# A four-layer network on one Trainium2 core: layer 3 gets its gate weights by DMA through memory, its output biases on VectorE, and eight units of first products ahead of the gate

## What is computed

```python
x_flat = x.transpose(0, 2, 3, 1).reshape(-1, c)
scores = softmax(x_flat @ gate_w + gate_b, -1)
top_v, top_i = top_k(scores, 2)
top_w = softmax(top_v, -1)                         # two weights for each pixel
present = (top_i[:, :, None] == arange(4)[None, None, :]).any(0)   # [2, 4], over all pixels
coef = einsum('ke,kbhw->ebhw', present, wmap)      # wmap: top_w as [2, b, h, w]
hdn = relu(einsum('bchw,edc->ebdhw', x, w1) + b1)
y   = einsum('ebdhw,eod->ebohw', hdn, w2) + b2
out = einsum('ebohw,ebhw->bohw', y, coef)
```

## Time and profile before

| | us |
|---|---|
| median of 3 runs | 5612.05 (5609.07 to 5618.05) |
| the profiled execution | 5612.2 |
| its span in the trace | 5610.3 |
| start of the last image's tail to the first second product | 4527 to 4596 |
| the loop over units, to the last matmul | 4596 to 5606 |

### The profile page before, as it was taken

One profiled execution on the slowest core, in us unless ns is written; L12 is line 12 of the kernel. 1 busy time (PEld: TensorE's weight loads), 2 busy tenths in 40 slices (PEclk: granted clock), 3 DMA queues, 4 the chain that ended last, 5 costly groups with the idle time before them and its releaser, 6 DMA issues. The chain is left out here.

```text
span 5610.3 us, 78498 instructions
## 1 busy us (share of the span) xinstructions
PE 4822.8 (86%) x28644; PEld 3822.7 (68%) x28644; DVE 4242.3 (76%) x4727; ACT 3094.3 (55%) x6442; POOL 2967.4 (53%) x3548
## 2 busy tenths in 40 slices
PE   4888888888888888888888877788887979999999
PEld 2666666666666666666666654466665859999998
DVE  1999999999999999999999986666666643333333
ACT  3776777777777777777777743222232323333332
POOL 3776777777777777777777744545443400000000
PEclk8999999999999999999999988798887979999999
DMA  2001000000000010000000012102010101000100
GB/s 74 1 15 29 9 9 10 9 22 22 10 9 10 19 29 14 9 9 10 9 9 10 5 41 80 43 19 75 28 37 15 64 25 33 28 26 28 33 26 22
DMA packets 88527, 136.75 MB, mean 24 GB/s; under 512 B 5285, under 2 KB 85185, under 8 KB 88141
## 3 DMA queue, kind: packets, MB, share of 16 engines
q1 hardware_dynamic: 88140, 131.72, 7.3%
HBM read 89.23 MB, written 42.47 MB: 23 GB/s over the span
## 5 line engine op out<-in xcount | busy, mean ns | idle before, releaser
L743 DVE TENSOR_TENSOR_SCAN a_h<-a_dA,pw 128x771 f32<-128x771 f32 x1152 | 2014.1, 1751 | 121.7 <-PE pw L450 120.8
L599 ACT ACTIVATE a_dA<-a_dt,a_Aneg 128x384 f32<-128x384 f32 x2304 | 1345.2, 607 | 152.4 <-DVE a_h L743 147.4
L461 PEld LDWEIGHTS pw<-g_ident,a_h 128*128 128x128 f32 x6912 | 783.5, 142 | 618.2 <-DVE a_acc L762 268.1
L881 POOL TENSOR_SCALAR a_dBT<-a_dtxT,a_BC 128x768 f32<-128x768 f32 x1152 | 1025.0, 907 | 298.4 <-PE pw L450 213.7
L461 PE MATMUL pw<-g_ident,a_h 128*128 128x128 f32 x6912 | 980.6, 279 | 227.7 <-DVE a_acc L762 157.8
L450 PE MATMUL pw<-g_ident,a_dBT 128*128 128x128 f32 x6912 | 954.2, 275 | 4.8 <-POOL a_dBT L881 4.8
L762 DVE SCALAR_TENSOR_TENSOR a_acc<-pw,a_BC,a_acc 128x768 f32<-128x768 f32 x912 | 913.8, 1002 | 50.9 <-PE pw L461 46.7
L450 PEld LDWEIGHTS pw<-g_ident,a_dBT 128*128 128x128 f32 x6912 | 801.5, 142 | 6.6 <-POOL a_dBT L881 5.5
L1895 DVE TENSOR_TENSOR d_hf<-d_hf,ps 128x384 f32<-128x384 f32 x288 | 159.1, 554 | 566.0 <-ACT d_hf L1825 555.5
L833 POOL TENSOR_TENSOR a_xin<-a_xin,a_tm 128x384 f32<-128x384 f32 x432 | 433.0, 1002 | 34.3 <-ACT a_tm L520 9.0
L893 POOL TENSOR_TENSOR a_acc<-a_acc,a_tm 128x768 f32<-128x768 f32 x168 | 307.0, 1827 | 161.1 <-ACT a_tm L613 160.2
(11 more groups left out here) (243 smaller groups left out, 9365.2 us busy)
## 6 DMA issues: line engine op xcount, KB each, us to landing
b_xs<-x SPq DMA_DIRECT2D x36, 576.0 KB, 4.0
a_xs<-in_x SPq DMA_DIRECT2D x24, 576.0 KB, 4.0
x<-a_xs SPq DMA_DIRECT2D x24, 576.0 KB, 3.0
b_x<-x SPq DMA_DIRECT2D x24, 576.0 KB, 4.6
e_xs<-x SPq DMA_DIRECT2D x24, 576.0 KB, 3.9
out<-e_xs SPq DMA_DIRECT2D x24, 576.0 KB, 3.0
a_sx<-in_x SPq DMA_DIRECT2D x54, 192.0 KB, 2.4
x<-b_x SPq DMA_DIRECT2D x16, 576.0 KB, 3.0
```

The costliest lines, as they stand in the source:

```text
L461: t = e.transpose(m["pw2"][:, c * 128:(c + 1) * 128], m[f"a_h{g % 2}"][:, c // 2, first_col(c) + tb * 128:first_col(c) + (tb + 1) * 128], ...
L599: e.activation(dA[:, first_col(c):first_col(c) + T], m[f"a_dt{k % 2}"][:, c, :], ACT.Exp, scale=m["a_Aneg"][:, c, n:n + 1]).then_inc(s["a_ ...
L743: e.tensor_tensor_scan(m[f"a_h{g % 2}"][:, p % 3, :], m[f"a_dA{pi % NDA}"][:], m[f"pw{pi % 2}"][:, COL:COL + PAIR], 1.0, ALU.mult, ALU.add ...
L881: t = e.tensor_scalar(m[f"a_dBT{g % 2}"][:, tb, :], m[f"a_dtxT{o}"][:, tb, :], m[f"a_BC{o}"][:, tb, n:n + 1], 1.0, ALU.mult, ALU.mult)
```

## The change

- **Weights.** The gate's result lies as `e_co`, expert by expert. TensorE turns it once, with three transposes, into 96 x 384 in `ps3`; ScalarE copies that to `e_cT`; one DMA writes it to a new tensor `cw` in memory (144 KB). For each chunk one DMA reads 4 x 384 weights and spreads them over all 128 partitions into one of three buffers `d_wb` (768 KB written). `scale3_dve` reads that instead of PSUM. The 96 matmuls of `weigh_pe`, the 72 transposes of `by_expert_pe` and 23 of 24 copies on ScalarE go.
- **Biases.** The 72 bias matmuls go. `bias3_dve` adds weight times b2 to `e_xs` with three VectorE operations of 128 x 384 in each unit, 288 in all, after `scale3_dve` of the next unit and ahead of the final additions.
- **Gate.** 26 VectorE operations, most on all four experts at once (128 x 288, with repeated operands), in place of 64. Three operations that prepared b2, and four ScalarE operations (selection, b2, two copies to `e_cs`), go. GpSimd sets four constants `g_rank`.
- **Ahead.** NAHEAD is 8: 24 groups of first products stand ahead of the gate's matmuls, and `d_hf` has 24 buffers. They reach into chunk 1, so `pre3_dve`, `pre3_act` and the load of chunk 1 come ahead of the last image's tail. In the loop the first product of unit u + 1 still stands just ahead of the second product of unit u, from u = 7 on; the second products of units 0 to 6 follow each other.

```diff
 NU = NCH * NEXP
-NAHEAD = 3
+NAHEAD = 8
+NHF = 3 * NAHEAD
...
-def weigh_pe(e, m, w, M, u):
-    k, x = divmod(u, NEXP)
-    M.claim("v_gs", 3 * (u + 1))
-    w.wait_ge("a_cT", k + 1)
-    w.wait_ge("a_pk", 2)
-    e.matmul(m["ps3"][:, 0:T], m["d_pickr"][:, x, :], m[f"e_cT{k % 2}"][:], start=True, stop=True).then_inc(m.s["pe_wg"], 1)
-
-
 def combine_pe(e, m, w, u):
     k, x = divmod(u, NEXP)
-    o = k % 2
     for c in range(CT):
         ps, col = outs3(m)[c], slice(x * C + c * 128, x * C + (c + 1) * 128)
         if x == 0:
             w.wait_ge("v_yo", 3 * (k - 1) + c + 1)
-            w.wait_ge("v_b2r", 3)
-            e.matmul(ps, m["d_b2r"][:, c * 128:(c + 1) * 128], m[f"e_cT{o}"][:], start=True, stop=False, skip_group_check=True)
         for i in range(3):
             w.wait_ge("v_hl", 3 * u + i + 1)
             for z, (A, B) in enumerate((("W2h", "hh"), ("W2l", "hh"), ("W2h", "hl"))):
-                t = e.matmul(ps, m[f"c_{A}"][:, i, col], m[f"e_{B}{u % 2}"][:, i, :], start=False, stop=x == 3 and i == z == 2, skip_group_check=True)
+                t = e.matmul(ps, m[f"c_{A}"][:, i, col], m[f"e_{B}{u % 2}"][:, i, :], start=x == 0 and i == 0 and z == 0, stop=x == 3 and i == z == 2, skip_group_check=True)
...
-    by_expert_pe(e, m, w, M, 0)
-    weigh_pe(e, m, w, M, 0)
+    M.claim("a_cT", 1)
+    w.wait_ge("v_sm", GATE_END)
+    for g in range(3):
+        t = e.transpose(m["ps3"][0:96, g * 128:(g + 1) * 128], m["e_co"][:].rearrange("p x n -> p (x n)")[:, 96 * g:96 * (g + 1)], m["g_ident"][:])
+    t.then_inc(m.s["pe_cT"], 1)
     for u in range(NU):
-        k, x = divmod(u, NEXP)
-        if u + 1 < NU:
-            if x == 2 and k + 1 < NCH:
-                by_expert_pe(e, m, w, M, k + 1)
-            weigh_pe(e, m, w, M, u + 1)
-            if u + 1 >= NAHEAD:
-                for i in range(3):
-                    hidden_pe(e, m, w, 3 * (u + 1) + i)
+        if NAHEAD <= u + 1 < NU:
+            for i in range(3):
+                hidden_pe(e, m, w, 3 * (u + 1) + i)
         combine_pe(e, m, w, u)
...
+    pre3_act(e, m, w, 1)
     march([tail_act(e, m, w, NB - 1)], 3 * NAHEAD, lambda n: relu_act(e, m, w, n))
-    e.activation(m["d_pickr"][:].rearrange("p e n -> p (e n)"), m["d_pick"][:, 0:512], ACT.Copy).then_inc(s["a_pk"], 1)
-    e.activation(m["d_b2r"][:], m["d_b2"][:], ACT.Copy).then_inc(s["a_pk"], 1)
     l12_over(w)
     w.wait_ge("v_sm", GATE_SUB)
     e.activation(m["g_coef"][:], m["g_coef"][:], ACT.Exp).then_inc(s["a_e1"], 1)
     w.wait_ge("v_sm", GATE_EQ)
     e.activation(m["e_eq"][:], m["e_eq"][:], ACT.Exp).then_inc(s["a_e2"], 1)
-    w.wait_ge("v_sm", GATE_END)
-    e.activation(m["e_cs"][:, :, 0:4], m["g_coef"][:], ACT.Copy).then_inc(s["a_cs"], 1)
-    e.activation(m["e_cs"][:, :, 8:12], m["g_coef"][:], ACT.Copy).then_inc(s["a_cs"], 1)
-    by_expert_act(e, m, w, 0)
+    w.wait_ge("pe_cT", 1)
+    e.activation(m["e_cT"][0:96, :], m["ps3"][0:96, 0:T], ACT.Copy).then_inc(s["a_cT"], 1)
     high_act(e, m, w, 0)
...
 def scale3_dve(e, m, w, u):
-    w.wait_ge("pe_wg", u + 1)
+    k, x = divmod(u, NEXP)
+    w.wait_ge(f"d_wb{k % 3}", 16 * (k // 3 + 1))
     for i in range(3):
         hi = 3 * u + i
-        f = m[f"d_hf{hi % 9}"]
+        f = m[f"d_hf{hi % NHF}"]
         w.wait_ge("a_hf", hi + 1)
-        e.tensor_tensor(f[:], f[:], m["ps3"][:, 0:T], ALU.mult).then_inc(m.s["v_gs"], 1)
+        e.tensor_tensor(f[:], f[:], m[f"d_wb{k % 3}"][:, x, :], ALU.mult).then_inc(m.s["v_gs"], 1)
...
+def bias3_dve(e, m, w, u):
+
+    k, x = divmod(u, NEXP)
+    for c in range(CT):
+        y = m[f"e_xs{k % 3}"][:, c, :]
+        w.wait_ge("v_xn3", 3 * (k + 1))
+        w.wait_ge("v_yb", 3 * (u - 1) + c + 1 if x > 0 else 0)
+        e.scalar_tensor_tensor(out=y, in0=m[f"d_wb{k % 3}"][:, x, :], scalar=m["d_b2"][:, c, x:x + 1], in1=y, op0=ALU.mult, op1=ALU.add).then_inc(m.s["v_yb"], 1)
...
     w.wait_ge("a_w", 6)
+    w.wait_ge("v_s", UNITS * NB)
     pre3_dve(e, m, w, 0)
+    pre3_dve(e, m, w, 1)
     march([tail_dve(e, m, w, NB - 1)], 0)
...
     gate3_dve(e, m, w)
+    w.wait_ge("d_l3", 16 * 2)
     scale3_dve(e, m, w, 0)
     for u in range(NU):
         k, x = divmod(u, NEXP)
         if u + 1 < NU:
-            if x == 2 and k + 1 < NCH:
+            if x == 2 and 2 <= k + 1 < NCH:
                 pre3_dve(e, m, w, k + 1)
             scale3_dve(e, m, w, u + 1)
+        bias3_dve(e, m, w, u)
         if x == 3:
             xs = m[f"e_xs{k % 3}"]
             for c in range(CT):
                 w.wait_ge("pe_cmb", 3 * u + c + 1)
-                e.tensor_tensor(xs[:, c, :], xs[:, c, :], outs3(m)[c], ALU.add).then_inc(s["v_yo"], 1)
+                w.wait_ge("v_yb", 3 * u + c + 1)
+                e.tensor_tensor(xs[:, c, :], xs[:, c, :], outs3(m)[c], ALU.add).then_inc(m.s["v_yo"], 1)
...
+    def weights(k):
+
+        w.wait_ge("v_yb", 3 * NEXP * (k - 2))
+        w.wait_ge("v_gs", 3 * NEXP * (k - 2))
+        e.dma_start(m[f"d_wb{k % 3}"][:], d["cw"].rearrange("(x n) t -> x (n t)", x=NEXP)[:, k * T:k * T + T].partition_broadcast(128)).then_inc(s[f"d_wb{k % 3}"], 16)
+
     w.wait_ge("v_wl", 6)
     load(0)
     w.wait_ge("pe_s", UNITS * NB)
-    for n in ("b1", "b2", "pick"):
+    w.wait_ge("v_s", UNITS * NB)
+    load(1)
+    for n in ("b1", "b2"):
         e.dma_start(m[f"d_{n}"][:], d[n]).then_inc(s["d_l3"], 16)
-    load(1)
     l12_over(w)
     load(2)
+    w.wait_ge("a_cT", 1)
+    e.dma_start(d["cw"].rearrange("(g r) t -> r g t", r=96), m["e_cT"][0:96, :].rearrange("r (g t) -> r g t", g=3)).then_inc(s["d_cw"], 16)
+    w.wait_ge("d_cw", 16)
+    weights(0)
+    weights(1)
     for k in range(NCH):
+        if k + 2 < NCH:
+            weights(k + 2)
```

More of the change, by code:

```diff
@@ L285, in place @@
     m.new("e_xs2", [128, 3, T])
[L286 to L289, removed]
+    m.new("e_cT", [128, T])
+    for n in ("mx", "v1", "cum", "eq", "cu"):
         m.new(f"e_{n}", [128, NB * NT])
     m.new("e_wk", [128, 2, NB * NT])
-    m.new("e_fk", [128, 2, 4, NB * NT])
+    m.new("e_fk", [128, 2, NB * NT, 4])
+    for n in ("eq4", "pr4"):
+        m.new(f"e_{n}", [128, NB * NT, 4])
+    m.new("e_co", [128, 4, NB * NT])
     m.new("e_fl", [128, 8])
@@ L304, in place @@
     m.new("e_xl1", [128, 3, T], F32R)
-    for i in range(9):
+    for i in range(24):
         m.new(f"d_hf{i}", [128, T])
+    for i in range(3):
+        m.new(f"d_wb{i}", [128, 4, T])
     return m
@@ L1906, in gate3_dve @@
+GATE_SUB, GATE_EQ, GATE_FLAGS, GATE_FB, GATE_END = 2, 17, 19, 23, 26
 def gate3_dve(e, m, w):
-    s, coef, mx, v1, cum, eq, wk, fk, fl, fb = m.s, m["g_coef"], m["e_mx"][:], m["e_v1"][:], m["e_cum"][:], m["e_eq"][:], m["e_wk"], m["e_fk"], m["e_fl"], m["e_fb"]
-    sc = [coef[:, :, x] for x in range(NEXP)]
+    s, coef, mx, v1, cum, eq, wk, fk, fl, fb = m.s, m["g_coef"], m["e_mx"], m["e_v1"], m["e_cum"], m["e_eq"], m["e_wk"], m["e_fk"], m["e_fl"], m["e_fb"]
+    eq4, pr4, co, cu = m["e_eq4"], m["e_pr4"], m["e_co"], m["e_cu"]
+    N = NB * NT
+    X = mybir.AxisListType.X
@@ L1925, in gate3_dve @@
[L1925 to L1930, removed]
-        w.wait_ge("v_sm", n)
[L1932 to L1945, removed]
+    each = lambda t: t.unsqueeze(2).broadcast_to([128, N, NEXP])
@@ new lines, in gate3_dve @@
+    e.tensor_reduce(mx[:], coef[:], X, ALU.max).then_inc(s["v_sm"], 1)
+    w.wait_ge("v_sm", 1)
+    e.tensor_tensor(coef[:], coef[:], each(mx[:]), ALU.subtract).then_inc(s["v_sm"], 1)
+    w.wait_ge("a_e1", 1)
+    e.tensor_reduce(v1[:], coef[:], X, ALU.add).then_inc(s["v_sm"], 1)
+    w.wait_ge("v_sm", 3)
+    e.reciprocal(v1[:], v1[:]).then_inc(s["v_sm"], 1)
+    w.wait_ge("v_sm", 4)
+    e.tensor_tensor(coef[:], coef[:], each(v1[:]), ALU.mult).then_inc(s["v_sm"], 1)
+    for k, n in ((0, 5), (1, 11)):
+        w.wait_ge("v_sm", n)
+        e.tensor_reduce(wk[:, k, :], coef[:], X, ALU.max).then_inc(s["v_sm"], 1)
+        w.wait_ge("v_sm", n + 1)
+        e.tensor_tensor(eq4[:], coef[:], each(wk[:, k, :]), ALU.is_equal).then_inc(s["v_sm"], 1)
+        w.wait_ge("v_sm", n + 2)
+        w.wait_ge("p_const", 4 + NDA + NEXP)
+        e.tensor_tensor(pr4[:], eq4[:], m["g_rank"][:].unsqueeze(1).broadcast_to([128, N, NEXP]), ALU.mult).then_inc(s["v_sm"], 1)
+        w.wait_ge("v_sm", n + 3)
+        e.tensor_reduce(cu[:], pr4[:], X, ALU.max).then_inc(s["v_sm"], 1)
+        w.wait_ge("v_sm", n + 4)
+        e.tensor_tensor(fk[:, k, :, :], pr4[:], each(cu[:]), ALU.is_equal).then_inc(s["v_sm"], 1)
@@ L1946, in gate3_dve @@
         if k == 0:
-            for x in range(NEXP):
-                e.scalar_tensor_tensor(out=sc[x], in0=fk[:, k, x, :], scalar=-2.0, in1=sc[x], op0=ALU.mult, op1=ALU.add).then_inc(s["v_sm"], 1)
-    e.tensor_tensor(eq, wk[:, 1, :], wk[:, 0, :], ALU.subtract).then_inc(s["v_sm"], 1)
+            w.wait_ge("v_sm", 10)
+            e.scalar_tensor_tensor(out=coef[:], in0=fk[:, 0, :, :], scalar=-2.0, in1=coef[:], op0=ALU.mult, op1=ALU.add).then_inc(s["v_sm"], 1)
+    w.wait_ge("v_sm", 16)
```

(2 more changed lines are left out.)

98 lines of the change are left out of this document (32 added, 66 removed).

## The result

| | us | span of the profiled execution |
|---|---|---|
| before, median of 4 runs | 5615.05 (5609.07 to 5620.83) | 5610.3 |
| changed, median of 4 runs | 5490.68 (5480.82 to 5492.17) | 5487.2 |

The ratio is 0.9775, 95% interval 0.9758 to 0.9792: 2.25% less time; the two medians are 124.4 us apart. The forecast was 5490, with 5480 to 5508 as its range.

A forecast was written before the change was run, and what follows sets the result against it. TensorE bounds the loop, the gate's chain the stretch ahead. First second product at 4617.3, plus 826.3 and 37.6 of products, 2.2 clock, 0.5 wait, 4.1 behind and 1.9 around the span: 5490 us, range 5480 to 5508.

The forecast's parts named there:

- The loop: Loop over units: TensorE's 4.94 us besides products go from each of 24 chunks, 118.6 us in all, without new steady waits.
- VectorE's biases: Loop: 12 biases a chunk on VectorE at 0.60 us each, 7.2 us, making 23.5 of 37.56 us, covered.
- Eight units ahead: Ahead of the gate: exponential queued behind all relus, so 15 added groups move 23.5 us of work and save none.
- The wait of the tail: Before the gate: TensorE waits 2.3 us for the last image's averages, as chunk 1 is split first.
- The gate: VectorE's gate operations behind the exponential take 10.9 us, to 4606.0; repeated operands could add 1 us.
- Through memory: Gate weights through memory: write of 144 KB 2.9 us, read of 768 KB 4.5 us, to 4615.3.
- The clock after the gate: First second products: low clock for 4.7 us, costing 2.2 us; bounds 0 and the old 16.4 us (+7.5).
- (a): Low clock again 16 us (+5.3), reads share (+3.6) or bias dear (+5): 5493 to 5504; 82% together with the forecast.
- (b): Loop: VectorE is late, two biases' time in a unit returns as a wait; +48 us, 5538; 6%.
- (e): Loop: only the start gains, TensorE's 4.94 us return as small gaps at each unit; +96 us, 5586; 3%.
- (c): Gate hides behind the products after all, though the lists exclude all but 1.2 us; fast side 5484; 5% below 5480.
- (d): SyncE's queue: the read spreading one row over 128 partitions becomes the bound; 5668 us at 45 us a read; 4%.

The follow-up runs named there:

- small96: Changed kernel plus one unused 12-row matmul at the head of each of the 96 second products; 5549.69 us, ratio 0.9881 to before.
- before_no_bias: Kernel before without its 72 bias matmuls (b2 left out); 5574.38 us, ratio 0.9927 to before.
- no_bias: Changed kernel without `bias3_dve`, 288 VectorE operations less (b2 left out); 5493.96 us, ratio 0.9774 to before.
- bias_twice: Changed kernel with three more VectorE operations of the bias's kind in each unit, result unread; 5498.09 us, ratio 0.9788 to before.
- ahead3: Changed kernel with NAHEAD = 3, chunk 1 split in the loop as before; 5498.34 us, ratio 0.976 to before.
- gate_early: Changed kernel with the gate's ScalarE and TensorE steps put among the first products ahead; 5474.58 us, ratio 0.9723 to before.
- read_alone: Changed kernel with the weight reads for chunks 1 and 2 issued only after the first scaling; 5504.35 us, one run.
- old_gate: Changed kernel with the gate's separate VectorE operations for each expert put back (63); 5501.28 us, ratio 0.9772 to before.
- small_as_before: Changed kernel plus five unused 12-row matmuls in the first two second products, laid as in the kernel before; 5493.20 us, one run.
- small_start: Changed kernel plus one 12-row matmul at each group of nine in units 0 to 3, 12 in all; 5494.46 us, ratio 0.9779 to before.

## Why the prediction was right, point by point

- **The loop.** Forecast: 4.94 us less in each chunk, no new wait. Measured: 42.50 to 37.47, 5.03, and no wait; the 0.5 us that the forecast had for one in units 0 to 6 did not come either, where each second product starts 4.68 us after the one before. What a small matmul costs with the restart of the stream behind it, 0.57, is confirmed by small96 (0.573) and before_no_bias (0.58). The term was 2.2 us short over the loop, because the pace of 9.39 us for 54 matmuls, 0.1739 each, was read from the last piece of the chain of waits; inside the loop the changed kernel ran at 37.47 / 216 = 0.1735.
- **VectorE's biases.** 0.60 us was taken, 0.610 measured for one; as they overlap at their ends, the 288 keep VectorE busy for 160.1 us, 0.556 each, and they cost nothing (no_bias). Looking at the order was needed: in bias_twice as much work again costs 7.4 us in the first seven units (4.7 of a wait, 2.7 of the clock), where there is only one product to a unit, and nothing in the loop.
- **Eight units ahead.** The step that carried most of the judgement, that the exponential stands behind all relus and so nothing of the gate is hidden, is shown from both sides: ahead3 (0.7 us) and gate_early (23.3 us).
- **The wait of the tail.** Mis-sized: 2.3 us forecast (its own numbers give 4532.2 - 4530.1 = 2.1). TensorE did wait for VectorE's averages, for 1.80 us by the timeline, but the last gate logits came only 0.7 us later from chunk 0. The clock was granted at 1.00 from 6.9 to 10.3 us from chunk 0, where before it was at 0.50 until 13.1; the averaging matmuls took 1.88 us instead of 2.98. The prediction allowed for a longer low clock there (0 to +2 us), not for a shorter one.
- **The gate.** 10.9 us for VectorE, 10.8 measured. Repeated operands cost nothing: each such operation took 0.46 us, as the plain one of the earlier trace rows. The two flag reductions took 1.22 us instead of 0.81, with four-element strides now; the one with two operators 0.46 instead of 0.53.
- **Through memory.** Both sizes were off and cancelled, which is luck: the write 1.9 for 2.9, the read 5.5 for 4.5. I had scaled the read by its bytes from plain loads; read_alone shows that this read is slower by itself. The two DMAs take back more than the gate's shorter chain won: 5 us won (old_gate), 7.4 us for the DMAs. The estimate of 6.1 us for the two, worked out in the prediction from the Trainium skill (DMA: Bandwidth & Descriptors, Anatomy of one DMA), is 1.3 too low; the fit in that section is for DMAs issued by GpSimd, and these are issued by SyncE.
- **The clock after the gate.** 4.7 us at half clock forecast for +2.2 us, 3.8 us after the first second product measured, and 1.8 lost (the next first product starts 34.6 us after the first second product, 32.8 at full clock). The 0.32 us that the sum took for a matmul at half clock is 0.35 in the rows of small_as_before (3.18 for nine). The reasoning behind the short stretch did not hold as a rule: small_start has 12-row matmuls at each group and rises as early. The Trainium skill (TensorE: Matmul & The Clock Gate, Part 1) says that the clock falls when the engine stands; the traces agree: in gate_early TensorE stands for 1.7 us only, and the granted clock is 1.00 from 13.7 us after chunk 0 to the end of the loop.
- **The rivals.** (a) did not happen, except for the read's +1.0. (b) and (e) are out by a loop with no idle time. (c) was excluded by the lists and then built as gate_early. (d), the spreading read as a bound: 5.7 us to landing in the loop (median of 19), against the 43 at which it would have decided.

## What to carry to other kernels

A small matmul inside a saturated stream costs more than its own duration: here 0.37 us in the row, 0.57 in the time, and 168 of them with 24 turns and waits were 2% of a kernel. If another engine has slack on the same operands and the data can come by DMA two steps ahead, move it there, and check the order of that engine's work, not only its sum. Work put ahead of a serial chain hides the chain only if the chain's own steps stand among that work in every engine's list: look for the first step that is queued behind it (here one exponential behind 24 relus, 23 us).

## What the runs showed of the hardware that I had not expected

- After TensorE had been idle, half clock lasted 16.1 to 16.3 us beyond the first full matmul in three traces of two kernels with 12-row matmuls between the first groups of nine, and 3.0 to 6.2 us in nine others, two of which (small_start, small96) have such matmuls as well. In small_as_before that cost 5.4 us over and above the small matmuls.
- A DMA that spreads 4 rows of 1536 bytes over 128 partitions (768 KB written) takes 5.3 us to landing, alone, and 5.5 to 5.8 with two like it behind it; plain loads of 576 KB take 3.9 and 3.8 in the same loop. The store of a chunk takes 5.8 us beside such reads and took 3.0 before, off the path in both.
- One pause of TensorE of 4.7 us in the middle of products (bias_twice) brought its clock down to 0.5 for 6.8 us and cost 2.7 us on top.
- A write of 144 KB to memory lands in 1.9 us, less than any load or store of the earlier trace rows.
